# Four unread products ahead of each mask, earlier statistics in the first stage, and a last store in two pieces

## The reference

```python
def _L0_gnn_ref(x, edge_index, W, att_src, att_dst, bias):      # loops added: src, dst of 53125 edges
    xp = (x @ W).reshape(N, H, C)
    a_src = jnp.einsum('nhc,hc->nh', xp, att_src)
    a_dst = jnp.einsum('nhc,hc->nh', xp, att_dst)
    ...
    e = jax.nn.leaky_relu(a_src[src] + a_dst[dst], NEG_SLOPE)
    m = jax.ops.segment_max(e, dst, num_segments=N)
    ee = jnp.exp(e - m[dst])
    z = jax.ops.segment_sum(ee, dst, num_segments=N)
    out = jax.ops.segment_sum(xp[src] * (ee / z[dst])[:, :, None], dst, num_segments=N)
    return jax.nn.relu(out.reshape(N, H * C) + bias)

def _L1_gnn_ref(x, W, a, src, dst):
    h = x @ W
    e = jnp.exp(-jax.nn.leaky_relu((h @ a[0, :d])[src] + (h @ a[0, d:])[dst], negative_slope=0.1))
    rowsum = jax.ops.segment_sum(e, src, num_segments=N)
    h_prime = jax.ops.segment_sum(e[:, None] * h[dst], src, num_segments=N)
    return jax.nn.elu(h_prime / (rowsum[:, None] + EPS))

h = jnp.maximum(_layernorm(x, axis=-1), 0.0)
x = x + _L0_gnn_ref(h, ...)
h = jnp.maximum(_layernorm(x, axis=-1), 0.0)
x = x + _L1_gnn_ref(h, ...)
```

## Time and profile before

| | us |
|---|---|
| median of 3 runs | 2246.73 |
| lowest, highest | 2242.46, 2251.78 |
| the profiled execution, time | 2247.59 |
| its span, first to last instruction | 2245.7 |

### The profile page before, as it was taken

How to read it: one execution, slowest core, us unless ns; L and a number is a source line. 1 busy time by engine, 2 the same in 40 slices (tenths; PEclk the granted TensorE clock), 3 DMA queues, 4 the chain that set the end, 5 groups by cost and what they waited for, 6 DMA issues and landing times. The chain is left out here.

```text
span 2245.7 us, 27642 instructions
## 1 busy us (share of the span) xinstructions
PE 1727.7 (77%) x10226; PEld 934.6 (42%) x10226; DVE 1137.3 (51%) x2763; ACT 400.8 (18%) x791; POOL 1356.3 (60%) x1296
## 2 busy tenths in 40 slices
PE   3757838569742788888889888834999998998995
PEld 2323414224321455545455455511444544454554
DVE  5635817457631566666767676752333333333331
ACT  1111201112100121222112222211112121222211
POOL 1555566675776576667666666207666776677630
PEclk9878958788875778777777777766899999999998
DMA  7211302213118999999999999629999999999961
GB/s 226 67 51 48 90 26 83 55 31 117 54 38 312 321 349 345 350 368 364 341 353 357 360 366 364 203 92 412 381 367 354 362 361 355 353 358 350 358 211 42
DMA packets 186942, 561.15 MB, mean 250 GB/s; under 512 B 45693, under 2 KB 50146, under 8 KB 186448
## 3 DMA queue, kind: packets, MB, share of 16 engines
q0 software_dynamic: 139776, 416.40, 51.6%
q1 hardware_dynamic: 43428, 129.78, 16.9%
q10 hardware_dynamic: 3600, 13.16, 1.5%
HBM read 554.33 MB, written 53.28 MB: 271 GB/s over the span
## 5 line engine op out<-in xcount | busy, mean ns | idle before, releaser
L930 POOL DMA_INDIRECT ring<-layer_rows,idx x360 | 402.7, 1119 | 233.7 <-PE acc L1055 111.5
L412 POOL DMA_INDIRECT src_lists<-pay_T,slot_T x392 | 405.1, 1033 | 221.1 <-issue 128.7
L1489 POOL DMA_INDIRECT ring<-layer_rows,idx x360 | 373.6, 1038 | 177.2 <-issue 96.3
L508 PE MATMUL mm<-w_sb,hT 128*128 128x512 f32 x800 | 389.5, 639 | 26.9 <-issue 26.5
L1055 PE MATMUL acc<-ring,weight 128*32 128x256 f32 (+1 forms) x3600 | 343.9, 484 | 9.6 <-issue 5.5
L508 PEld LDWEIGHTS mm<-w_sb,hT 128*128 128x128 f32 x800 | 161.8, 208 | 220.4 <-issue 220.4
L1551 PE MATMUL acc<-ring,weight 128*32 128x512 f32 x1600 | 215.2, 620 | 37.4 <-issue 36.6
L1055 PEld LDWEIGHTS acc<-ring,weight 128*32 128x32 f32 (+1 forms) x3600 | 152.5, 137 | 140.8 <-issue 97.7
L1651 DVE TENSOR_TENSOR hT_low<-tp_l,hT_high 128x512 fp32r<-128x512 f32 x50 | 34.6, 691 | 281.9 <-issue 205.7
L1584 PE MATMUL mm_l<-w_high,hT_high 128*128 128x512 f32 x400 | 168.8, 422 | 8.4 <-issue 6.2
L1022 PE MATMUL wide<-score_T,spread 16*128 16x128 f32 x800 | 154.3, 337 | 22.5 <-issue 22.4
(11 more groups left out here) (232 smaller groups left out, 2131.9 us busy)
## 6 DMA issues: line engine op xcount, KB each, us to landing
layer_rows<-row_l ACTq DMA_DIRECT2D x25, 514.0 KB
layer_rows<-row_l SPq DMA_DIRECT2D x25, 514.0 KB
own<-layer_rows SPq DMA_DIRECT2D x25, 512.0 KB
x<-xb SPq DMA_DIRECT2D x25, 512.0 KB
x1t<-x SPq DMA_DIRECT2D x25, 512.0 KB
xt<-in_x_dram SPq DMA_DIRECT2D x24, 512.0 KB
xb<-in_x_dram SPq DMA_DIRECT2D x24, 512.0 KB
out_dram<-y SPq DMA_DIRECT2D x24, 512.0 KB
```

What stands on the lines that cost most here:

```text
L412: pool.indirect_dma_start(out=list_d, out_offset=bass.IndirectOffsetOnAxis(ap=slot_T[:, b:b + 1], axis=0), in_=pay_T[:, b:b + 1], in_offse ...
L508: last = pe.matmul(mm[k][:, f * HALF:(f + 1) * HALF], hT[k][:, c, :], w_sb[:, c, f * HALF:(f + 1) * HALF], start=c == 0, stop=c == KC - 1)
L930: pool.indirect_dma_start(out=ring[:, t % 2, blocks(c), :][:, q, :], out_offset=None, in_=table0, in_offset=bass.IndirectOffsetOnAxis(ap=i ...
L1489: pool.indirect_dma_start(out=fetched(t, c)[:, q, :], out_offset=None, in_=table1, in_offset=bass.IndirectOffsetOnAxis(ap=idx, axis=0), bo ...
```

## The change

Three edits, in three stages.

1. In `attend`, for every tile but the first, four products of the bf16 identity with itself, spread to 128x512, go into `wide[r % 2]` ahead of the mask's product. The mask's product starts the bank anew, so nobody reads them. They stand behind the same waits as the mask's product did: 5 rounds x 24 tiles x 4 = 480 products.
2. In the first stage `mv`, `std`, `rstd` and `nbias` get two buffers, and `statistics` is cut in two: the part up to `bn_aggr` stays first in DVE's tile; the reciprocal and the bias are `rescale`. The slots of the chunks come between the two, one turn of the loop later in the text. The wait for `h_done` of the same tile goes; `rescale` waits for that of two tiles earlier.
3. In `collect`, the last tile's 53 rows are stored as 48 rows and 5 rows, in two transfers one after the other on SP's queue.

```diff
@@ lists_and_project
-        mv = sb("mv", [P, 2])
+        mv = [sb(f"mv_l0_{k}", [P, 2]) for k in range(2)]
...
             def statistics(i):
                 k = i % 2
                 dve.wait_ge(x_in[k], 16 * (i // 2 + 1))
+                if i >= 1:
+                    dve.wait_ge(aggr_done, i)
                 for j in range(2):
                     dve.bn_stats(stats[:, j, :], xt[k][:, j * HALF:(j + 1) * HALF]).then_inc(stats_done, 1)
                 dve.wait_ge(stats_done, 2 * i + 2)
-                dve.bn_aggr(mv[:, :], stats[:, :, :].rearrange("p a b -> p (a b)")).then_inc(aggr_done, 1)
+                dve.bn_aggr(mv[k][:, :], stats[:, :, :].rearrange("p a b -> p (a b)")).then_inc(aggr_done, 1)
+
+            def rescale(i):
+                k = i % 2
                 dve.wait_ge(std_done, i + 1)
-                dve.reciprocal(rstd[:, :], std[:, :]).then_inc(rstd_done, 1)
+                if i >= 2:
+                    dve.wait_ge(h_done, i - 1)
+                dve.reciprocal(rstd[k][:, :], std[k][:, :]).then_inc(rstd_done, 1)
                 dve.wait_ge(rstd_done, i + 1)
...
-                dve.wait_ge(h_done, i + 1)
...
             for i in range(TILES):
                 if i + 2 < TILES:
                     statistics(i + 2)
+                for c in chunks_of(i - 2):
+                    slot_chunk(c)
+                if i + 2 < TILES:
+                    rescale(i + 2)
                 for c in chunks_of(i):
                     rank_chunk(c)
...
                 score(i)
-                for c in chunks_of(i - 1):
-                    slot_chunk(c)
@@ attend
+    BUSY = 4
...
+                if t >= 1:
+
+                    for _ in range(BUSY):
+                        pe.matmul(wide[r % 2][:, :, :], ident16[:, :],
+                                  ident16[:, :].rearrange("p (o n) -> p o n", o=1).to_broadcast([P, H, P]),
+                                  start=True, stop=True, skip_group_check=True)
                 pe.matmul(wide[r % 2][:, :, :], ident16[:, :],
@@ collect
+    EVEN = TAIL // 16 * 16
...
-                size = TAIL if t == TILES - 1 else P
-                sp.dma_start(rows(out, t, size), y[0:size, :]).then_inc(y_out, 16)
-            sp.wait_ge(y_out, 16 * TILES)
+                if t < TILES - 1:
+                    sp.dma_start(rows(out, t), y[:, :]).then_inc(y_out, 16)
+                else:
+                    sp.dma_start(out[t * P:t * P + EVEN, :], y[0:EVEN, :]).then_inc(y_out, 16)
+                    sp.dma_start(out[t * P + EVEN:N, :], y[EVEN:TAIL, :]).then_inc(y_out, 16)
+            sp.wait_ge(y_out, 16 * (TILES + 1))
```

More of the change, by code:

```diff
@@ L185, in lists_and_project @@
         stats = sb("stats", [P, 2, 6])
-        mv = sb("mv", [P, 2])
-        std = sb("std", [P, 1])
-        rstd = sb("rstd", [P, 1])
-        nbias = sb("nbias", [P, 1])
+        mv = [sb(f"mv_l0_{k}", [P, 2]) for k in range(2)]
+        std = [sb(f"std_l0_{k}", [P, 1]) for k in range(2)]
+        rstd = [sb(f"rstd_l0_{k}", [P, 1]) for k in range(2)]
+        nbias = [sb(f"nbias_l0_{k}", [P, 1]) for k in range(2)]
         prod = sb("prod", [P, C])
@@ L434, in normalise @@
                 act.wait_ge(aggr_done, i + 1)
-                act.activation(std[:, :], mv[:, 1:2], ACT.Sqrt, bias=eps[:, :]).then_inc(std_done, 1)
+                act.activation(std[k][:, :], mv[k][:, 1:2], ACT.Sqrt, bias=eps[:, :]).then_inc(std_done, 1)
                 act.wait_ge(norm_done, i + 1)
@@ L438, in normalise @@
                     act.wait_ge(h_used, 2 * (i - 1))
-                act.activation(ht[k][:, :], xt[k][:, :], ACT.Relu, bias=nbias[:, :], scale=rstd[:, :])\
+                act.activation(ht[k][:, :], xt[k][:, :], ACT.Relu, bias=nbias[k][:, :], scale=rstd[k][:, :])\
                     .then_inc(h_done, 1)
@@ L567, in statistics @@
                 dve.wait_ge(stats_done, 2 * i + 2)
-                dve.bn_aggr(mv[:, :], stats[:, :, :].rearrange("p a b -> p (a b)")).then_inc(aggr_done, 1)
+                dve.bn_aggr(mv[k][:, :], stats[:, :, :].rearrange("p a b -> p (a b)")).then_inc(aggr_done, 1)
+            def rescale(i):
+                k = i % 2
                 dve.wait_ge(std_done, i + 1)
-                dve.reciprocal(rstd[:, :], std[:, :]).then_inc(rstd_done, 1)
+                if i >= 2:
+                    dve.wait_ge(h_done, i - 1)
+                dve.reciprocal(rstd[k][:, :], std[k][:, :]).then_inc(rstd_done, 1)
                 dve.wait_ge(rstd_done, i + 1)
-                dve.scalar_tensor_tensor(out=nbias[:, :], in0=mv[:, 0:1], scalar=-1.0, in1=rstd[:, :],
+                dve.scalar_tensor_tensor(out=nbias[k][:, :], in0=mv[k][:, 0:1], scalar=-1.0, in1=rstd[k][:, :],
                                          op0=ALU.mult, op1=ALU.mult).then_inc(norm_done, 1)
-                dve.wait_ge(h_done, i + 1)
             def score(i):
@@ L696, in _ @@
             statistics(0)
+            rescale(0)
             dve.wait_ge(iota_set, 3)
@@ L713, in _ @@
             statistics(1)
+            rescale(1)
             first_rows()
```

## The result

| | before | changed |
|---|---|---|
| median of the runs, us | 2246.52 | 2296.38 |
| lowest, highest | 2242.46, 2251.78 | 2288.95, 2300.27 |
| the profiled execution, time (span) | 2247.59 (2245.7) | 2300.27 (2298.5) |

The ratio is 1.0226, with a 95% interval of 1.0185 to 1.0267. The changed kernel is slower by 2.3%; the forecast was 2229 us, in a range from 2205 to 2252.

A forecast was written before the change was run, and what follows sets the result against it. The prediction took PE to pace stage one and transfers, with PE close behind, to bound stage two. From the profiled 2247.6 us, -8.5 (store), -5 (first stage), -4.5 (products), less 0.9 to the median, gave 2229 us; range 2205 to 2252.

The forecast's parts named there:

- The last store: At the end, splitting 53 rows into 48 and 5 cuts SP's wait from 10.4 to 1.9 us: -8.5 us.
- The first stage: DVE no longer waits before `mine`, mostly hidden behind a busy PE: -5 us, bounds -24 to +13.5.
- the one that the prediction had set aside: First stage: PE's longest wait for `hT`, 21.9 us, excluded because PE's own small products crept there; 24.3 us left.
- The products: Stage two: 480 added products, 115 us of PE work at the upper clock, net -4.5 us, bounds -12 to +5.
- as long as the clock passes 0.83: Stage two: condition on the products' gain; PE outruns the transfers only above mean clock 0.83, up from 0.77.
- enough transfers are queued that the engines stay full: Stage two: POOL's 125.4 us standing for `add_rows` was said to leave the DMA engines full, except between 1423 and 1434.
- where the share is 1.00, nothing: Stage two: the products were said to gain nothing where the DMA share is 1.00.
- Rival A: Stage two: the clock stays, PE becomes the bound, +56 us, 2289 us in all; chance 0.13.
- the dip near 1423: Stage two, 1423 to 1434, DMA share 0.52: 5.3 us of transfers missed, of which 4 counted as gain.
- POOL's wait for `acc`: Stage two: expected below 125 us as a sign that the products work.
- The net nothing of the tail: Behind the last gather, 1441 to 1480: up to 4.9 us saved by PE's speed, 4.8 added by products, net nothing.

The follow-up runs named there:

- e8: The kernel before with only the last store split into 48 and 5 rows; ratio 0.9946 to the kernel before.
- second group: Four follow-up kernels run together on a second chip, where the kernel before took 2245.32 us.
- e1: The changed kernel without its 480 products, earlier statistics and split store kept; ratio 0.9951 to the kernel before.
- e6: The changed kernel with no products ahead of the masks, 12 per tile ahead of `turn(t + 1, 3)`; ratio 0.9876 to the kernel before.
- e9: The changed kernel with 20 products per tile ahead of `turn(t + 1, 3)`, none ahead of the masks; 2069.08 us against 2102.51 for the kernel before.
- e7: The changed kernel with eight products ahead of each mask in place of four; ratio 1.018 to the kernel before.

## Why the prediction was wrong

**The last store: right.** Forecast -8.5; the time from the last `y` to the end fell by 8.0, SP's wait is 1.8 us against the 1.9 worked out, and e8's interval holds it. The rule of the Trainium skill (DMA: Bandwidth & Descriptors, "Why a DMA increments its semaphore by 16 and not by 1") was the right one to go by, and the trace agrees: the window behind the issue has a share of 0.57 at 132 GB/s, where one engine gave 0.06 and 22.

**The first stage: right in sign, and small, as said.** Forecast -5, within -24 to +13.5. The last scatter came at 668.7 instead of 675.9. In the second group it came at 657.6 to 661.2 with the edit and at 665.4 without, in the first at 609.3 to 610.7 with and 610.9 without. So it is worth 0 to 8 us, as single traces show it. In the ratios it can't be told apart from nothing (e1 0.9951 with both edits, e8 0.9946 with the store alone). PE's wait for `hT` fell from 46.2 to 18.4 us. Without the longest of each (21.9 and 3.5 us), the one that the prediction had set aside, it fell by 9.4, which is near the 7.2 us at the end of the stage; that the one became the other is not shown.

**The products: the clock right, the time wrong.** The forecast was -4.5 within -12 to +5, "as long as the clock passes 0.83". It passed, at 0.86, and the stage became 65 us longer. The step that failed stands in what bounds the kernel: "enough transfers are queued that the engines stay full", and in the working: "where the share is 1.00, nothing". I read a DMA share of 1.00 as transfers that can't go faster, and so took POOL's 125.4 us for `add_rows` as covered. The evidence against it lay in my own rows: in the earlier trace rows a share of 1.03 goes with 411 GB/s, and in the earlier trace rows 1.00 with 353. At 411 the 30.6 us of a tile would be 26.3 (30.6 x 353 / 411). That is an estimate of what lay between the transfers and what happened, some 4 us a tile; no run kept 411 GB/s up over a whole tile. POOL's wait, 5.5 us a tile (125.4 over 23), was large enough to hold them back. e6 and e9, at 365 and 362 GB/s with the same data, show that the transfers had room, if only 2 to 3% of it. The share didn't show it: it is 1.00 in both the kernel before and e9, from 800 to 1350.

What the runs showed in its place is the loop: in a stage whose DMA share is 1.00, work between the landing and the release of the places lengthens each tile, here from 30.6 to 33.2 us. With that step mended, the price could have been read from the rows of the kernel before. The stretch behind the wait is in the earlier trace rows, 1025.0 to 1031.5 at 0.50, and four products at the lower clock are twice the 0.96 us of the forecast: 1.9 us a tile for round 2, and up to 2 for rounds 3 and 4, at 24 tiles 46 to 94. Measured: 65.

**Rival A** came near in time (2289 against 2296) but not in its mechanism. Its condition was a clock that stays at 0.77 and PE as the bound. The clock rose, and PE sat idle for 110 of 700 us. It would have been wrong to count the result as its confirmation, and e7 shows what it would have led to: by its reckoning twice the products cost another 115 us or more of PE, and the kernel was not slower at all.

**The other terms.** Of the 4.5 us forecast for the products, 4 were to come from the dip near 1423. It wasn't filled: in the changed kernel it lies 58 us later, and the 11 us from 1481 to 1492 have a share of 0.45 at 133 GB/s. POOL's wait for `acc`, which was to fall below 125 us, rose to 151.0. The products' busy time is 151.9 us, not 115: they were priced at the upper clock, and a part of them ran at the lower. The net nothing of the tail could not be seen separately. Layer 1, which I had left alone, is 2.8 us longer, which I don't explain.

What stays open: which releases set the tile. The way from the landing to `add_rows(t, 3)` goes with it in the kernels that keep the order, but not one for one (in e9 1.9 us less of the way, 1.1 us less of the tile). Nor does the total of POOL's wait follow the tile: from 800 to 1350 it is 111.2 us in e9 and 104.9 in e1, though e9's stage is the shorter. Between 12 and 20 products in the wait none were tried, nor was a ring of more than 10 places.

## What to carry to other kernels

A share of busy time near 1 on the DMA engines is no proof that they are the limit; compare the GB/s of windows, and don't write off a wait of the engine that issues the transfers where it recurs in each tile. Its total is no price, though: it names the loop, and an experiment has to say what the loop costs. Where transfers, work and the release of buffers form a loop, look first at the way from landing to release: the same 20 products a tile cost 60 us where most of them stood behind the landing, and gave 23 us ahead of it. Filling work for the clock belongs into the wait itself, and a mean clock over the stage tells nothing of the clock on that way.

## What the runs showed of the hardware

- **The same share, other rates.** In one tile of the changed kernel the DMA engines moved 302 GB/s at a share of 1.04 in a stretch in which POOL issued gathers, and 411 at 1.03 in one in which it mostly stood.
- **The clock behind busy stretches.** In e9 PE was busy and at the upper level from 1017.9 to 1025.9 and idle for 1 us; the next 3.5 us, of nothing but 128x512 products, were granted 0.63:

```profile
1017.90:1021.40 3.50, 3.48 (x45) 2.42 (x45) 2.28 (x4) 0.39 (x2) 2.89 (x3) 1.00 1.00 374
1021.40:1025.90 4.50, 4.46 (x51) 2.90 (x50) 1.71 (x4) 0.10 (x1) 3.30 (x4) 1.00 1.03 372
1025.90:1026.90 1.00, 0.00 (x1) 0.01 (x1) 0.93 (x3) 0.00 (x0) 0.99 (x1) 1.00 1.06 298
1026.90:1030.40 3.50, 3.50 (x11) 1.36 (x12) 3.23 (x10) 0.00 (x0) 2.59 (x4) 0.63 1.03 291
```

  The Trainium skill (TensorE: Matmul & The Clock Gate, "What's actually happening") ties the lower clock to idleness. The changed kernel's fall in a wait of 4.13 us agrees; this one, behind 1 us of it, asks for more, and so did the first fall of the earlier trace rows.
- **Four and eight products at one price.** 1.91 us for four and 1.89 for eight, by the clock alone.
- **The same kernel, 143 us apart on two chips.** It took 2103.0 and 2102.5 us in the two groups that ran on one chip, and 2245.3 us in the group on the other. By e1's and e8's traces (139 us apart) 55 us of it are in the first stage, 76 in layer 1, and 9 in the stage whose loop this study is about. What differs between the chips no run shows.
